# A graph-layer kernel: edge ranks from equality inside a partition plus a carry, edge-by-edge hits, gathers that wait on TensorE's own semaphore, edge lists loaded as strips

## What is computed

```python
h = jnp.maximum(_layernorm(x, axis=-1), 0.0)            # x: 12500 x 128, float32
src, dst = edge_index                                   # 200000 edges, sorted by dst
agg = segment_sum(h[src], dst, num_segments=12500)
deg = segment_sum(ones, dst, num_segments=12500)
agg = agg / jnp.maximum(deg, 1.0)[:, None]
t = relu(agg @ Wg + h @ Ws + bg)                        # 128 x 128 each
t = tanh(t @ W1 + b1)                                   # 128 x 512
t = tanh(t @ W2 + b2)                                   # 512 x 512
out = x + t @ W3 + b3                                   # 512 x 128
```

## Time and profile before

| | us |
|---|---|
| median of 3 runs | 2292.16 (2290.43 to 2300.48) |
| the profiled execution, its own time | 2291.04 |
| its span, first to last instruction | 2288.7 |
| mean granted TensorE clock | 0.807 of full |

### The profile page before, as it was taken

The page is one execution under the profiler, slowest core; times in us unless marked ns, Lnnn a source line. Parts: engine busy times, 40 slices in busy tenths (PEclk is TensorE's granted clock), DMA queues, the critical chain, the costliest instruction groups (busy, mean ns, idle before and its releaser), DMA issues.

```text
span 2288.7 us, 25107 instructions
## 1 busy us (share of the span) xinstructions
PE 1508.0 (66%) x8357; PEld 1126.4 (49%) x8357; DVE 1073.5 (47%) x2596; ACT 561.2 (25%) x1167; POOL 990.3 (43%) x1043
## 2 busy tenths in 40 slices
PE   0021866576767777667686766777776766786678
PEld 0011754354545455555465544455545554564457
DVE  2461754454355454355354535355535552555331
ACT  1351313031223131123131313131313130322132
POOL 7336054635352535352534363534363255225430
PEclk9955878688778787788787888787879787888799
DMA  6131021121211121211122121122121212111210
GB/s 219 67 110 48 9 75 44 44 64 52 62 47 53 49 64 49 66 42 56 50 63 72 30 77 36 49 62 71 31 65 49 61 41 81 27 55 51 72 39 8
DMA packets 86476, 132.16 MB, mean 58 GB/s; under 512 B 23893, under 2 KB 65497, under 8 KB 82649
## 3 DMA queue, kind: packets, MB, share of 16 engines
q0 software_dynamic: 33024, 67.70, 11.1%
q1 hardware_dynamic: 49110, 61.26, 8.3%
q10 hardware_dynamic: 4226, 1.63, 0.3%
HBM read 117.50 MB, written 13.01 MB: 57 GB/s over the span
## 4 chain that ended last, share of the span: by engine, by line
PE 49%; another core or an unknown queue 25%; issue 13%; DVE 8%; ACT 4%; DMA 0%; DVEq 0%; SPq 0%; ACTq 0%
PE banks L829 13%; PE banks L795 11%; PE banks L780 7%; PE banks L814 6%; PE banks L704 5%; PE banks L753 2%; PE banks L841 2%; DVE arena L1261 1%; DVE onehot L1394 1%; PE banks L853 1%; DVE arena L1553 1%; ACT dense L1126 1%; ACT arena L1147 1%; ACT outT L1133 1%
## 5 line engine op out<-in xcount | busy, mean ns | idle before, releaser
L613 POOL DMA_INDIRECT ring<-h_table,idx_slot x968 | 928.0, 959 | 1213.4 <-DVE idx_slot L1465 861.9
L829 PE MATMUL banks<-dense,w 128*128 128x256 f32 (+1 forms) x1568 | 432.3, 398 | 25.9 <-ACT dense L1126 13.4
L829 PEld LDWEIGHTS banks<-dense,w 128*128 128x128 f32 x1568 | 279.6, 201 | 69.1 <-ACT dense L1126 14.1
L795 PE MATMUL banks<-arena 128*128 128x257 f16 x1666 | 249.9, 313 | 73.8 <-issue 73.1
L1147 ACT CAST arena<-banks 128x512 f16<-128x512 f32 (+1 forms) x425 | 237.6, 579 | 247.2 <-PE banks L780 136.2
L780 PE MATMUL banks<-xin,arena 128*128 128x256 f16 (+1 forms) x1666 | 239.9, 276 | 65.0 <-DVE arena L1553 50.5
L704 PE MATMUL banks<-ring,onehot 128*128 x1121 | 238.9, 299 | 24.6 <-issue 24.0
L1564 DVE TENSOR_SCALAR arena<-node,qd 128x256 f16<-128x256 f16 x833 | 173.1, 291 | 169.7 <-PE banks L795 79.6
L795 PEld LDWEIGHTS banks<-arena 128*128 128x128 f16 x1666 | 182.6, 111 | 138.3 <-issue 96.2
L780 PEld LDWEIGHTS banks<-xin,arena 128*128 128x128 f16 (+1 forms) x1666 | 158.4, 99 | 114.7 <-DVE mean_rows L1591 43.4
L841 PE MATMUL banks<-dense,w 128*128 128x256 f32 x392 | 139.2, 483 | 85.4 <-ACT dense L1126 64.4
(11 more groups left out here) (140 smaller groups left out, 1357.9 us busy)
## 6 DMA issues: line engine op xcount, KB each, us to landing
arena<-unit_codes SPq DMA_DIRECT2D x17, 1568.0 KB
ring<-h_table,idx_slot POOLq DMA_INDIRECT x968
xin<-in_x_dram SPq DMA_DIRECT2D x6, 1024.0 KB, 5.6
h_table<-xin SPq DMA_DIRECT2D x6, 1024.0 KB, 3.8
tblk<-h_table SPq DMA_DIRECT2D x48, 128.0 KB
xblk<-in_x_dram SPq DMA_DIRECT2D x48, 128.0 KB
out_dram<-dense SPq DMA_DIRECT2D x48, 128.0 KB
arena<-in_x_dram,arena POOLq DMA_INDIRECT x64
```

The lines of the kernel that those rows point to most:

```text
L613: nc.gpsimd.indirect_dma_start(out=ring_tiles[:, k * GT + j, 0:2 * D], out_offset=None, in_=table, in_offset=bass.IndirectOffsetOnAxis(ap= ...
L795: mm = nc.tensor.matmul(unit_ps[h][:, 0:2 * D + 1], wide[:, (NP + p) % WSLOTS, g - lo, h * P:(h + 1) * P], unit_msgs[:, g, 0:2 * D + 1], s ...
L829: mm = nc.tensor.matmul(l3_ps[c][:, 0:w], w2[:, q, c * P:(c + 1) * P], h2T[:, q, 0:w], start=(q == 0), stop=(q == HC - 1))
```

## The change

- **Ranks.** The prefix sum goes. `count_earlier` compares, inside each partition, the group of every edge with those of the 35 edges before it (36 x 36 comparisons, filled with -1 at the front) and adds up, in three halvings or reductions: the number of earlier edges of the same group. `rank_edges` multiplies the hits with the carry of each group, adds halves, reduces over 25 columns and adds the earlier count. The four instructions of `take_carry`, `scan_places` and the old `rank_edges` go.
- **Hits edge by edge.** `hits` is laid out [edge, group] with 50 columns, `oh_pay` [edge, k, group], so that the 98 values of an edge lie side by side for `place_chunk`. `count_groups` adds halves twice and leaves 9 rows of counts; `carry_groups` is then 9 matmuls of 49 columns instead of 2.
- **The carry** is copied by ACT (`take_carry` in its slot 9) instead of DVE.
- **Gathers.** `idx_slot`, `fill_idx` and `idx_ready` go. POOL reads `idx_all` directly, waits on `seg_done` itself, at the same step as before, and its loop is unrolled.
- **Order on DVE.** In a period, `count_earlier` stands between masks 5 and 6; `rank_edges` and the first two `spread_ranks` come before the second step; `match_nodes` 0 and 1 after it; the window's lead is loaded for the next step at the end of the one before. At the period's end three of the four first masks of the next unit are made before `finish_unit`, one behind it.
- **Order on PE.** In short periods `place_chunk` 0 and 1 stand inside `layer3` at slot 9 instead of behind it.
- **Edge lists** are loaded as 120 strips of 1664 edges, one for each partition, and one rest; the copies after the turn write with a stride of 13.

```diff
-            def gather_pair(pair, k):
-                wait_alone(pool, idx_ready, pair - RAWG // 2 + 1, issuing)
-                gather_group(2 * pair, k)
-                gather_group(2 * pair + 1, k + 1)
-            with pool.Fori(1, GROUPS // RG) as i:
...
+            for pair in range(RAWG // 2, GROUPS // 2):
+                if pair >= RAWG:
+                    wait_alone(pool, seg_done, pair - 5, issuing)
+                gather_group(2 * pair)
+                gather_group(2 * pair + 1)
...
-                nc.tensor.matmul(carry_ps, before16[:], group_count[:, 1:HI + 1], start=True, stop=False)
-                nc.tensor.matmul(carry_ps, upto16[:], group_count[:, 0:HI], start=False, stop=True).then_inc(carry_done, 1)
+                for t in range(UT // 4):
+                    mm = nc.tensor.matmul(carry_ps, before16[:], group_count[:, t, 0:HI], start=(t == 0), stop=(t == UT // 4 - 1))
+                mm.then_inc(carry_done, 1)
...
-                                          oh_pay[:, :, :, c * CT + t].rearrange("p k g -> p (k g)"),
+                                          oh_pay[:, c * CT + t].rearrange("p k g -> p (k g)"),
...
+            def count_earlier(n):
+                at(dve, wide_ready, 2 * NP * (n - 1) + WSLOTS + 2)
+                nc.vector.tensor_tensor(earlier, group_of.unsqueeze(1).to_broadcast([P, UT, UT]), group_before, ALU.is_equal
+                                        ).then_inc(earlier_ready, 1)
...
+                nc.vector.tensor_tensor(earlier[:, 0:half], earlier[:, 0:half], earlier[:, half:UT], ALU.add
...
+                nc.vector.tensor_tensor(earlier[:, 0:quarter], earlier[:, 0:quarter], earlier[:, quarter:half], ALU.add
...
+                nc.vector.tensor_reduce(earlier_sum[:], earlier[:, 0:quarter].rearrange("p d t -> p t d"), AX.X, ALU.add
...
             def rank_edges(n):
                 dve.wait_ge(carry_taken, n + 1)
+                nc.vector.tensor_tensor(hits, hits, carry16[:].unsqueeze(1).to_broadcast([P, UT, HG]), ALU.mult
...
+                nc.vector.tensor_tensor(hits[:, :, 0:HG // 2], hits[:, :, 0:HG // 2], hits[:, :, HG // 2:HG], ALU.add
...
+                nc.vector.tensor_reduce(rank_ps, hits[:, :, 0:HG // 2], AX.X, ALU.add).then_inc(rank_ready, 1)
...
             def step(s):
-                dve.wait_ge(seg_done, s - 2)
-                if 2 * (s + 3) < GROUPS:
-                    fill_idx(s + 3, (s + 3) % 4)
                 finish(s)
...
                 match_nodes(n, [4, 5, 6, 7])
                 take_nodes(n + 1)
+                match_codes(n + 1, range(WSLOTS - 1))
                 finish_unit(n)
-                match_codes(n + 1, range(WSLOTS))
+                match_codes(n + 1, [WSLOTS - 1])
```

234 lines of the change are left out of this document (132 added, 102 removed).

## The result

The changed kernel takes 2301.73 us (median of 20 runs, 2295.58 to 2307.06), the kernel before 2293.35 us (20 runs, 2286.7 to 2300.48). The ratio is 1.0039, with a 95% interval of 1.0031 to 1.0047: slower by 8 us, where I had forecast 42 us faster. The profiled execution of the changed kernel spans 2302.0 us, 13.3 more than before's 2288.7.

A forecast was written before the change was run, and what follows sets the result against it. PE was taken as the engine that matters, held up by pairs of gathers. The terms 12 + 12 + 9 + 3 + 6 = 42 us gave 2291 - 42 = 2249, as median about 2250; range 2170 to 2300.

The forecast's parts named there:

- chunks 0 and 1: place_chunk 0 and 1 behind the third step of long periods: saving worth 0, since a release ends that stretch.
- The rival: In ten long periods an earlier fourth-step sum makes gather pairs run together: some 4 us lost each, 2310 us; chance 0.13.
- Bound and hold: A pair of gathers takes some 20 us, leaves PE free about 8, holds the others until about 3 after.
- Chunks 2 and 3: place_chunk 2 and 3, in front of a held stretch in ten long periods: 1.2 us each, 12 us saved.
- The end of a period: First masks made before the mean: PE starts 0.75 us earlier, 16 times, 12 us saved.
- POOL waits itself: Between step and gather a copy of 174 ns goes: 0.17 us for each of 53 pairs, 9 us saved.
- Prologue: Ahead of the periods: one gather starts 7 us earlier, taken as 3 us saved, bounds -5 and 8; strips 0.
- Short periods: PE's 6.06 us wait for the ranks ends, mostly inside a held stretch: 1 us for six periods, 6 us saved.
- DVE's work: DVE's instructions for a unit: 8 us added, 3 us less in all, within its idle time, so counted 0.
- The carry: 7 more matmuls of 49 columns, 0.4 us, before the held stretch behind the first step: 0, at most 6 us lost.
- Rival 1: Throughout the kernel PE's saved time counts wherever it lies: 130 us saved, 2161 us; chance 0.18.
- Rival 3: The stride isn't the cause, the masks are held, only POOL's index copies go: 2282 us; chance 0.12.

The follow-up runs named there:

- b_contig: Kernel before with the contiguous place_chunk operand alone, its writes strided and slow: 2346.16 us against 2317.98, ratio 1.0135.
- a_apart: Changed kernel plus one wait: the pair behind a long period's fourth step waits for place_chunk 3; 2254.69 us, ratio 0.9844 (1431.48 us where gathers delay nobody).
- b_end: Kernel before with the new order at the end of a period alone (three masks ahead of finish_unit, one behind): 2286.51 us, ratio 0.9874.
- b_gather: Kernel before with the gather part alone (POOL reads idx_all, waits on seg_done itself, loop unrolled): 2281.02 us, ratio 0.9839.
- b_contig2: Kernel before with the contiguous operand alone, written contiguously and read with a stride, on an occasion without gather delays: 1538.64 us, ratio 0.9687.
- a_again: The changed kernel itself, unaltered, measured again on an occasion without gather delays: 1430.49 us against 1590.21 for the kernel before.
- b_strips: Kernel before with the edge lists loaded as strips alone: 2311.97 us, ratio 0.9978.

## Why the prediction was wrong

**The step that failed** is "chunks 0 and 1 stand behind the third step, in a stretch that the release at 1142.4 ends: worth 0". The pace was right in kind (187 ns before; now 45 at full clock, a little under my 55), and that stretch does end with the gathers. But I priced a saving there as if its end were fixed. It isn't, because the end of the stretch also starts the next pair. In period 3 of before the fourth step's last matmul is recorded at 787.2, 13.0 us into the pair that began at 774.16; its sum is held until 797.5. In the changed kernel it is recorded at 767.1, 9.1 us into its pair, and seen at 768.63. The last rows of the sum on PE, of before and of the changed kernel:

```profile
786.82 0.39 PE L704 MATMUL banks<-ring,onehot 128*128 x2
```

```profile
766.72 0.39 PE L712 MATMUL banks<-ring,onehot 128*128 x2
```

Two things made it earlier. One is the chunks, 0.81 us instead of 3.36:

```profile
757.04 0.97 PE L762 MATMUL banks<-arena 128*128 128x98 f16 x18
757.85 2.39 PE L838 MATMUL banks<-dense,w 128*128 128x256 f32 x10
```

The other is in the windows of the ten matmuls behind them (start:end, span, busy PE, PEld, DVE, ACT, POOL, granted clock, DMA), of before and of the changed kernel:

```profile
776.30:780.10 3.80, 3.80 (x11) 2.97 (x11) 3.80 (x3) 0.31 (x1) 2.89 (x4) 0.55 0.14 35
```

```profile
757.80:760.10 2.30, 2.30 (x16) 1.95 (x14) 2.23 (x4) 0.43 (x2) 0.95 (x2) 1.00 0.10 29
```

The clock was at 0.55 behind the long chunks and at 1.00 behind the short ones, and the ten matmuls take 2.2 us and not 3.9. I had counted the chunks' 2.4 us and not these 1.6.

**The rival was the right one**, and was given 0.13. It said: two chunks less before the fourth step, its sum seen before the last gather is out, pairs run together, 2310. Measured 2302. That the number fits as well is luck: its sizes were off in a way that cancels. It let ten periods join, and five did; it asked 4 us for each and it was 8.9 (136.3 against 127.5 with the pairs apart). What I held against it, that results recorded 9 to 10 us into a pair were mostly still held, is true and was the wrong argument: it is true of the other four. There the sum is recorded 9.2 us into the pair (1127.4, pair from 1118.14) and is seen at 1140.85, behind its end:

```profile
1118.14 0.94 POOL L627 DMA_INDIRECT ring<-h_table,idx_all  x1 [9.78 <-PE banks L712]
1119.38 0.94 POOL L627 DMA_INDIRECT ring<-h_table,idx_all  x1 [0.30 <-issue]
...
1136.86 0.94 POOL L627 DMA_INDIRECT ring<-h_table,idx_all  x1 [0.30 <-issue]
1141.62 0.94 POOL L627 DMA_INDIRECT ring<-h_table,idx_all  x1 [3.82 <-remote]
```

What tells the two kinds apart stands in these rows and was in before's as well: in the pairs that let the sum through, the second gather starts 2.08 us behind the first (758.01 to 760.09; in before 774.16 to 776.24), in the others 1.24. The longer step comes once in every four pairs, 64 gathers, and a short period shifts it by two pairs, so that it falls on the third pair of periods 3, 4, 8, 9 and 13, the very five. It is not the tenth of a microsecond between 9.1 and 9.2 that decides: in b_contig the sum is recorded 8.9 us into the third pair in all nine long periods, and is seen 12.8 us in where the step is the longer one and 22.8 us in where it is not; in a_apart4 it is recorded 9.1 us in both in period 3 and in period 6, and seen after 10.6 and 22.6. In before the five have the longer step too, but the sum is recorded 11.4 to 13.1 us in, and is held to the end. So in these runs it takes both, the longer step and an early sum; why the hold begins later behind the longer step was only seen, not tested. Which pair of the four each period's third one is could be read from the trace of before; how early is early enough could not.

**Point by point.**
- *Bound and hold.* Right in the main: a_apart4 moved the gathers alone, and the release moved with them, 2.85 us behind the last. That single results get through on the way (791.71 above) was overlooked, and that the hold would be there on every occasion was assumed and is wrong. The rule of the Trainium skill that I set against the row ("SBUF — State Buffer", "Who interferes with whom": DMA never contends with a compute engine) isn't borne out where the hold is there: ACT and PE stand still in it for 8.69 and 25.01 us in period 3. It isn't refuted either, since no run tells the data of the gathers from their issue on GpSimd, and nothing in the runs without the hold speaks against it.
- *Chunks 2 and 3*, 12 us: they stand in front of the fourth pair's hold only where pairs are apart. With the pairs apart the ten long periods (all but the last one) sum to 1280.8 us against before's 1279.3: the five are 1.9 us shorter each, where I had said 1.2, and the four others 3.3 longer, so that nothing of this term can be told for certain. In the changed kernel it is lost in the joined pairs. (At the low clock 18 matmuls took 1.48 us, 82 ns each, where I had said 110.)
- *The end of a period*, 12 us: PE's wait is 1.52 instead of 2.34 us, ended by the mean, as said; alone it brought 8 us by the spans. The wait is right; the 12 us were too high, because the nine long periods of b_end are 6 us longer in sum than before's, while its six short ones win 8.5.
- *POOL waits itself*, 9 us: in period 6 POOL starts 0.77 us behind DVE's first row of the step (1117.37 to 1118.14) instead of 0.97 (1118.87 to 1119.84). The step is right and its sum was not: b_gather alone brought 9.7 us by the spans, but 6.6 of them lie ahead of period 0, and the whole rest of the kernel won 3, not 9.
- *Prologue*, 3 us with strips 0: 16.6. The term was mis-sized. The strips alone bring the first gather 4.8 us forward. I had said that the casts wait until ACT is free at 100 us, and had not asked why ACT is free so late: it had issued the loads itself until 26.6 us. The gather part brings the ring's second use 9.4 us forward (280.7 to 271.3), for which I had seen 7.7 of waiting and then bargained it down.
- *Short periods*, 6 us and the ends' 4.5: 16.1 in all, 2.7 each. The end of a period alone brought 1.4 of these (b_end) and the gathers 0.6 (b_gather); the 0.7 that are left for the early chunks are near the 1 us that I had given them.
- *DVE's work*: 6.5 us added where I took 8 (0.86 ns an element), off the path, right. Without the hold DVE is in the chain with 39% in b_contig2 and 5 or 6% in the changed kernel, so there it seems to count.
- *The carry*: 153 matmuls, 6.6 us, nothing to be seen of them. Right.
- *Rival 1*, PE's time adds up: false with the hold. Without it, it is the better account of the kernel before (the contiguous operand alone brings 52 us), though not of the changed one, where POOL is the bound in long periods.
- *Rival 3*, it doesn't do what it says: false, by the pace of `place_chunk` and PE's wait of 1.52 us (b_end).

With the pairs apart the kernel takes 2254.69, where the forecast was 2250. That is good in part by chance: the prologue and the short periods won some 20 us more than I had given them, and the four other long periods lost 13 that I can't explain.

**A version that is good on both kinds of occasion** is a_apart: 0.9844 of the kernel before with the hold (0.9815 to 0.9872), and 0.8998 (0.8986 to 0.9011), 0.9004 and 0.8987 without it, where it is not to be told from the changed kernel.

## To carry to other kernels

Time saved inside a stretch whose end is fixed by somebody else is not worth nothing: ask what the earlier result will start. If it starts the next burst of the very thing that holds everybody, put a wait in the way, here one on a semaphore that PE raises behind the stretch. And where a quarter of a chain has no named releaser, a profile may show an occasion and not the kernel: here the same program took 2290 or 1590 us, and the ratio of two kernels was 1.004 or 0.90.

## What the runs showed of the hardware

- Matmuls of 98 float16 columns that lie 72 bytes apart start every 187 ns at a granted clock of 0.92 and of 0.50 (before). With the columns side by side they start every 45 ns at a granted clock of 1.00 (757.04 to 757.85 for 18, changed kernel; 46 in b_contig) and every 82 ns at 0.50 (1142.35 to 1143.83).
- On some occasions indirect gathers on GpSimd delay what the other engines see of each other, for up to 33 us, until 2 to 5 us behind the last gather, with single results seen on the way; on others, on the same two chips, not at all. Gathers take 0.94 us each, 1.25 apart, in both, but for longer ones without the hold, six of 2.15 to 2.93 us in the prologue of a_again.
- In every fourth pair (11, 15, 19 and so on to 63) the step from the first gather to the second is 2.08 us and not 1.25, if the pair starts after a wait: 14 times in before and in the changed kernel, and without the hold in the three such pairs of a_again that do (31, 47, 59).
- Two DMA issues of 768 KB in pieces of 512 bytes keep ACT's queue 11.2 and 11.7 us (before), two of 780 KB in pieces of 6656 bytes 0.60 and 0.33 us (b_strips).
- DVE's product of 1764 float16 elements takes 2.0 us when read and written in order, 3.5 when read with a stride of 74 bytes and 8.0 to 8.6 when written with a stride of 72 or 196 bytes.
